# GpSimd's element operations written per block of 256 columns, in a decoder block whose recurrence runs on GpSimd

## The chip, the cores and the metric

One NeuronCore of a Trainium2 chip runs the whole kernel in one launch. The metric is the device time of one execution in microseconds (us). The engines are named as in the profile: PE is TensorE (PEld its weight load), DVE is VectorE, ACT is ScalarE, POOL is GpSimd, SP is SyncE, which here issues most DMAs. Each engine takes its own instructions in program order and waits on semaphores for the others.

## The reference, cut to what matters

```
x: 32 sequence steps x 256 tokens x 256 channels;  ctx: the same shape
# 1. attention stand-in: a complex recurrence along the 32 steps, per channel
c = exp(-exp(lmlg)) * exp(1j * theta)
state_n = c * state_(n-1) + x_n          # real part used
x = layernorm(x + Re(state) * x)
# 2. cross attention, 16 heads of 16 channels, over 256 context tokens
q = relu(x Wq + bq); k = relu(ctx Wk + bk); v = relu(ctx Wv + bv)
o = softmax(q k^T / 4) v + q
x = layernorm(x + ln_g * normalised(o) + ln_b)
# 3. eight experts; each token goes to the nearest of eight centroids
xn = rmsnorm(x) * scale; id = argmin |xn - centroid|^2
y = (a * silu(g)) down_w[id],  [a, g] = xn up_w[id]
out = layernorm(y + 2x)                  # skip inside the block and around it
```

## The kernel before, in words

A step handles one of the 32 sequence positions as an item of 256 tokens by 256 channels, held as [128 partitions, 2 token halves, 256 channels]; so most element operations have 512 columns. A first phase (recurrence, cross attention, routing) runs 37 software-pipelined steps, t = -2 to 34. In step t, GpSimd computes the recurrence for item t+3, PE and DVE do the scores and row maxima of item t, ACT the exponentials of item t-1, DVE the attention's division and norms of item t-2, and DVE, GpSimd and PE route item t-3 to its expert, with a scatter of its rows into buckets in DRAM. A second phase (`experts`, whose first tile DVE starts on at 868.0 us) loops over the buckets; the change doesn't touch it.

The order of the work is written out by hand: each engine has a `step(t)` that calls its pieces in a fixed order, DVE and PE and ACT along the heads h = 0 to 15. GpSimd's `step` is the list below line 772. In steady state, it runs:

1. the double product of the recurrence, `by_re` (L694): state times the pair of decays, 1024 columns;
2. `xw` (L752), the weighted row of item t-3, which ACT squares and sums into `nx`; then `x` plus the bias (L782);
3. `q_lo` (L770): q minus its rounded part `q_hi`, for the next item;
4. `dist<-cent_norm,nx` (L761, `offset`, 16 columns). DVE's `dist` (L1388, `pick` stage 0), the first step of the choice of an expert, waits for it;
5. the real part of the state (L702), two small norm instructions (L727, L729), the state's product (L710), `k_lo` (L770), the state's sum (L713), two more small ones;
6. the scatter's two indirect DMAs (L802), which wait for DVE's `slot` (L1425), the last step of the choice;
7. the state plus the new x (L720), then L727 and L729, for which DVE's `row` (L1258) waits, and four small ones (`rms`).

Two things hang on this list. DVE's `u` (L1266), `oq` (L1370) and `onehot_bf` (L1405) read two tiles of SBUF each and run while GpSimd works through points 1 to 5. And `k_lo` goes out to DRAM and comes back as `k_st` (SP, L585 and L586), which PE's first scores of the next item (L1004) wait for.

The GpSimd functions that the change touches, with line numbers as in the profile:

Of the kernel before, what the change touches and what calls it, by code (L numbers as in the profile page):

```python
# [5 lines left out]
F32 = mybir.dt.float32  # L6
# [4 lines left out]
ALU = mybir.AluOpType  # L11
# [3 lines left out]
P = 128  # L15
SEQ, TOK, C = 32, 256, 256
NCH = C // P
NTC = TOK // P
# [63 lines left out]
def build(nc, x, ctx_in, lmlg, theta, last_conv, Wq, bq, Wk, bk, Wv, bv, ln_g, ln_b, ffn_scale, centroids, up_w, down_w, out):  # L82
    stack = ExitStack()
    with stack:
        def sb(name, shape, dt=F32):
            return stack.enter_context(nc.sbuf_tensor(name, shape, dt))
# [4 lines left out]
        def sem(name):  # L91
            return stack.enter_context(nc.semaphore(name))
# [13 lines left out]
        scale_bc = sb("scale_bc", [P, C])  # L106
# [14 lines left out]
        def sb1(name, shape, dt=F32):  # L121
            return phase1.enter_context(nc.sbuf_tensor(name, shape, dt))

        state = sb1("state", [P, 2, NTC, C])
        by_re = sb1("by_re", [P, 2, NTC, C])
        xt = sb1("xt", [P, 2, NTC, C])
# [22 lines left out]
        x1 = sb1("x1", [P, 4, NTC, C])  # L149
# [6 lines left out]
        xw = sb1("xw", [P, NTC, C])  # L156
# [6 lines left out]
        b_bc = sb1("b_bc", [P, C])  # L163
        decay = sb1("decay", [P, 2, C])
        decay_im2, decay_re = decay[:, 0], decay[:, 1]
# [26 lines left out]
        row = sb1("row", [P, 2, NTC, ROWW])  # L192
# [33 lines left out]
        s = {n: sem(n) for n in names.split()}  # L226
# [36 lines left out]
        def active(item):  # L263
            return item.within(0, SEQ)
# [271 lines left out]
        with nc.Block() as block:  # L536
# [114 lines left out]
            def _(pool):  # L651
                g = nc.gpsimd
# [27 lines left out]
                pool.wait_ge(s["params"], PARAMS * 16)  # L680
                pool.wait_ge(s["setup_dve"], 11)

                both = [P, 2, NTC, C]
                re_b = decay_re.unsqueeze(1).to_broadcast([P, NTC, C])
                pair_b = decay[:, :, :].unsqueeze(2).to_broadcast(both)

                def conv_products(item):

                    if not active(item):
                        return  # L690
                    wait(pool, "conv", item - 1, 5)
                    if item.k == 1:
                        wait(pool, "x1_ok", item - 1, 2)
                    g.tensor_tensor(by_re[:, :, :, :], state[:, 0].unsqueeze(1).to_broadcast(both), pair_b, ALU.mult).then_inc(s["conv"], 1)  # L694

                def conv_real(item):

                    if not active(item):
                        return
                    wait(pool, "conv", item, 5, 1)  # L700
                    wait(pool, "u_ok", item - 1)
                    g.tensor_tensor(state[:, 0], by_re[:, 1], state[:, 1], ALU.subtract).then_inc(s["conv"], 1)  # L702

                def conv_imag(item, j):

                    if not active(item):
                        return
                    if j == 0:
                        wait(pool, "conv", item, 5, 2)
                        g.tensor_tensor(state[:, 1], state[:, 1], re_b, ALU.mult).then_inc(s["conv"], 1)  # L710
                    else:
                        wait(pool, "conv", item, 5, 3)
                        g.tensor_tensor(state[:, 1], state[:, 1], by_re[:, 0], ALU.add).then_inc(s["conv"], 1)  # L713

                def conv_input(item):
                    if not active(item):
                        return
                    wait_ring(pool, x_in[item.mod(2)], item, 2, 16)
                    wait(pool, "conv", item, 5, 4)
                    g.tensor_tensor(state[:, 0], state[:, 0], xt[:, item.mod(2)], ALU.add).then_inc(s["conv"], 1)  # L720

                def rstd(item, ready, per, mv, rs, done):

# [22 lines left out]
                def weigh(item):  # L746

                    if not active(item):
                        return
                    wait(pool, "x2_ok", item, 2)  # L750
                    wait(pool, "nx_ok", item - 1, 2)
                    g.tensor_tensor(xw[:, :, :], row[:, item.mod(2), :, 0:C], scale_bc[:, :].unsqueeze(1).to_broadcast([P, NTC, C]),  # L752
                                    ALU.mult).then_inc(s["xw_ok"], 1)

                def offset(item):

# [7 lines left out]
                def cut(item, src, hi, lo, ready, done, out):  # L764

                    if not active(item):
                        return
                    wait(pool, ready, item, 4)
                    wait_ring(pool, out[(item - 1).mod(2)], item - 1, 2, 32)
                    g.tensor_tensor(lo[:, :, :], src, hi[:, :, :].bitcast(F32), ALU.subtract).then_inc(s[done], 1)  # L770

                def step(t):
                    n, a, b = t + 1, t - 2, t - 3
                    first = t.k < 0
                    if first:
                        rstd(t + 2, "ln1", 4, mv1, rs1, "rstd1")
                    conv_products(t + 3)
                    weigh(b)
                    if active(a):
                        wait(pool, "x1_ok", a, 2)  # L780
                        wait(pool, "x1T_pe", a)
                        g.tensor_tensor(x1[:, a.mod(4)], x1[:, a.mod(4)], b_bc[:, :].unsqueeze(1).to_broadcast([P, NTC, C]),  # L782
                                        ALU.add).then_inc(s["x1b_ok"], 1)
                    if n.k > 0:
                        cut(n, q32[:, :, :], q_hi, q_lo, "q_ok", "q_cut", q_out)
                    offset(b)
                    conv_real(t + 3)
                    if not first:
                        rstd(t + 2, "ln1", 4, mv1, rs1, "rstd1")
                    conv_imag(t + 3, 0)  # L790
                    if n.k > 0:
                        cut(n, k32[:, :, :], k_hi, k_lo, "k_ok", "k_cut", k_out)
                    conv_imag(t + 3, 1)
                    rstd(a, "lnx", 4, mvx, rsx, "rstdx")
                    if active(b):

                        p = b.mod(2)
                        wait(pool, "slot_ok", b, SLOT)
                        wait(pool, "id_ok", b)
                        wait(pool, "rms", b, 4)  # L800
                        for c in range(NTC):
                            g.indirect_dma_start(out=buckets[:, :], out_offset=bass.IndirectOffsetOnAxis(ap=slot[:, p, c:c + 1], axis=0),  # L802
                                                 in_=row[:, p, c, :], in_offset=None, bounds_check=PAD - 1,
                                                 oob_is_err=False).then_inc(scat[p], 16)
                    conv_input(t + 3)
                    rstd(a, "ln2", 4, mv2, rs2, "rstd2")
                    rms(a)

                steps(pool, step)
                gpsimd2(pool)  # L810

# [648 lines left out]
```

## Time and profile before

| | |
|---|---|
| median of 3 runs | 1257.54 us (1252.96 to 1257.8) |
| the profiled execution's own time | 1257.0 us |
| its span, first to last instruction | 1255.2 us |
| PE busy | 1119.9 us (89%) |
| DVE busy | 942.7 us (75%) |
| POOL busy | 783.9 us (62%), 932 instructions |
| ACT busy | 669.9 us (53%) |

The span is what the profile's rows are measured in; 1.8 us lie around it. Shares are means over both phases: POOL is busy eight to nine tenths of the time through most of the first phase and three tenths in the second. A busy time of two neighbours on one engine can overlap by some hundredths of a microsecond, since an instruction's span begins when it is handed over; the distance from start to start is what one costs in a row of several.

### The profile page before, as it was taken

The numbers are of one execution on the slowest core, as the hardware profiler recorded it, in microseconds if no ns is written. First come the engines' busy times: TensorE is split into PE (matmuls) and PEld (weight loads), VectorE is DVE, ScalarE is ACT, GpSimd is POOL, SyncE is SP. The second block draws the span as 40 slices with busy tenths as digits, with TensorE's granted clock in tenths as the row PEclk, the third lists the DMA queues.
The fourth block names the chain that finished last, engine by engine and source line by source line (L and its number), as shares of the span: only waits on it lengthen the run. The fifth ranks groups of instructions, "written<-read, shape, count | busy, mean of one in ns | idle before, by whom it ended". The sixth has DMA issues, their size and how long they took to land.

```text
span 1255.2 us, 27516 instructions
## 1 busy us (share of the span) xinstructions
PE 1119.9 (89%) x8060; PEld 820.0 (65%) x8061; DVE 942.7 (75%) x2416; ACT 669.9 (53%) x1416; POOL 783.9 (62%) x932
## 2 busy tenths in 40 slices
PE   3799989999999998989999999752999999999996
PEld 2466666666666666656666666431888888888885
DVE  7558998988988998999898898763555555555553
ACT  4166776766667776767676777641222222222221
POOL 4637888888878988879888865561233333333333
PEclk9689999999989999999999999555999999999998
DMA  4676676665555565556556555042111111111110
GB/s 131 146 179 194 174 207 183 182 156 139 141 140 146 149 158 137 147 139 161 136 146 156 136 134 126 11 151 59 44 51 47 43 50 50 49 47 48 50 51 22
DMA packets 90826, 144.91 MB, mean 115 GB/s; under 512 B 12663, under 2 KB 78336, under 8 KB 84513
## 3 DMA queue, kind: packets, MB, share of 16 engines
q1 hardware_dynamic: 83616, 126.09, 38.6%
q0 software_dynamic: 6528, 16.99, 4.6%
q8 instruction: 55, 0.90, 0.3%
q10 hardware_dynamic: 576, 0.53, 0.2%
q14 instruction: 51, 0.41, 0.1%
HBM read 91.44 MB, written 53.03 MB: 115 GB/s over the span
## 4 chain that ended last, share of the span: by engine, by line
PE 45%; DVE 19%; POOL 15%; issue 10%; DMA 8%; SPq 2%; ACT 1%; POOLq 0%; DVEq 0%; ACTq 0%
PE Y L454 10%; PE G L422 8%; PE A L422 8%; DVE neg_max_sb L1243 7%; PE S L1004 3%; PE M L988 3%; DMA k_st<-k_pieces 3%; DMA k_pieces<-k_lo 3%; DVE oq L1370 3%; POOL buckets L802 2%; PE GT L432 2%; PE O L980 2%; POOL rs L729 2%; POOL by_re L694 2%; PE M L960 2%
## 5 line engine op out<-in xcount | busy, mean ns | idle before, releaser
L1243 DVE TENSOR_REDUCE neg_max_sb<-S 128x2 f32<-128x512 f32 x512 | 328.3, 682 | 71.0 <-PE S L1004 69.2
L864 ACT ACTIVATE probs<-T 128x512 f32<-128x512 f32 x512 | 277.9, 595 | 148.1 <-PE T L1017 136.8
L1004 PE MATMUL S<-k_st,q_st 48*128 48x256 f32 x1024 | 215.3, 321 | 46.3 <-DMA k_st<-k_pieces 27.8
L1004 PEld LDWEIGHTS S<-k_st,q_st 48*128 48x128 f32 x1024 | 147.3, 194 | 123.7 <-issue 53.5
L1017 PE MATMUL T<-q_st,k_st 49*128 49x256 f32 x1024 | 211.9, 321 | 9.8 <-ACT probs L864 8.1
L1017 PEld LDWEIGHTS T<-q_st,k_st 49*128 49x128 f32 x1024 | 148.0, 195 | 28.3 <-ACT probs L864 17.0
L399 ACT ACTIVATE gT<-GT 128x512 f32<-128x512 f32 x71 | 42.5, 599 | 209.4 <-PE GT L432 209.4
L980 PE MATMUL O<-probs,v_aug 128*32 128x256 f32 x2048 | 151.0, 416 | 0.7 <-ACT probs L864 0.7
L378 POOL DMA_INDIRECT out<-res,token x71 | 76.4, 1077 | 103.3 <-DVE res L499 98.8
L454 PE MATMUL Y<-dn_sb,gT 128*128 x568 | 134.2, 379 | 0.8 <-ACT gT L399 0.8
L802 POOL DMA_INDIRECT buckets<-row,slot x64 | 69.7, 1089 | 85.0 <-DVE slot L1425 74.8
L454 PEld LDWEIGHTS Y<-dn_sb,gT 128*128 128x128 f32 x568 | 107.5, 189 | 18.3 <-issue 1.0
L422 PE MATMUL G<-up_hi,xsT 128*128 x284 | 107.7, 420 | 1.2 <-DVE xsT L504 1.0
L422 PE MATMUL A<-up_hi,xsT 128*128 x284 | 107.1, 418 | 0.0
L383 POOL TENSOR_SCALAR rs<-mv 128x1 f32<-128x1 f32 x71 | 16.0, 226 | 142.4 <-DVE mv L528 142.2
L499 DVE TENSOR_SCALAR res<-y,mv,rs 128x256 f32<-128x256 f32 x71 | 29.4, 414 | 86.1 <-POOL rs L385 86.1
L980 PEld LDWEIGHTS O<-probs,v_aug 128*32 128x32 f32 x2048 | 56.5, 115 | 56.2 <-ACT probs L864 16.0
L694 POOL TENSOR_TENSOR by_re<-state,decay 128x1024 f32<-128x1024 f32 x31 | 73.4, 2366 | 1.2 <-DVE x L1330 0.9
L403 ACT ACTIVATE gate<-G 128x512 f32<-128x512 f32 x71 | 42.4, 597 | 58.7 <-PE G L422 58.7
L988 PE MATMUL M<-ctT,wk_sb 128*128 128x256 f32 x256 | 67.0, 407 | 6.1 <-issue 6.0
L1116 PE MATMUL M<-wv_sb,ctT 128*128 128x256 f32 x256 | 70.5, 399 | 0.0
L988 PE MATMUL M<-x1T,wq_sb 128*128 128x256 f32 x256 | 68.2, 411 | 0.8 <-ACT x1T L877 0.8
(184 smaller groups left out, 2541.1 us busy)
## 6 DMA issues: line engine op xcount, KB each, us to landing
q_st<-q_pieces SPq DMA_DIRECT2D x64, 256.0 KB
k_st<-k_pieces SPq DMA_DIRECT2D x64, 256.0 KB
xr<-buckets SPq DMA_DIRECT2D x71, 129.0 KB, 2.1
xt<-in_x SPq DMA_DIRECT2D x32, 256.0 KB, 6.3
ct<-in_ctx SPq DMA_DIRECT2D x32, 256.0 KB, 6.8
q_pieces<-q_hi SPq DMA_DIRECT2D x32, 256.0 KB, 2.1
q_pieces<-q_lo SPq DMA_DIRECT2D x32, 256.0 KB, 2.2
q_st<-q_pieces SPq DMA_DIRECT2D x64, 128.0 KB
```

The source lines that it names most:

```text
L378: g.indirect_dma_start(out=out_rows, out_offset=bass.IndirectOffsetOnAxis(ap=token[:, f.mod(2):f.mod(2) + 1], axis=0), in_=res[:, f.mod(2) ...
L422: last = t_.matmul(ps[:, :], xT[:, w, c * P:(c + 1) * P], src[:, bass.ds(off + c * 2 * HID, HID)], start=(k == 0), stop=(k == len(terms) - 1))
L454: last = t_.matmul(Y_ps[:, 0:C], gT[:, m.mod(2), c * P:(c + 1) * P], dn_sb[:, bass.ds(off + c * C, C)], start=(c == 0), stop=(c == HCH - 1))
L694: g.tensor_tensor(by_re[:, :, :, :], state[:, 0].unsqueeze(1).to_broadcast(both), pair_b, ALU.mult).then_inc(s["conv"], 1)
L802: g.indirect_dma_start(out=buckets[:, :], out_offset=bass.IndirectOffsetOnAxis(ap=slot[:, p, c:c + 1], axis=0), in_=row[:, p, c, :], in_of ...
L864: a_.activation(probs[:, h % 8].rearrange("p k t -> p (k t)"), T_ps[h % 2][:, :], ACT.Exp, scale=DH ** -0.5).then_inc(s["exp_ok"], 1)
L980: last = t_.matmul(O_ps[32 * j:32 * j + 32, (grp % 2) * TOK:(grp % 2 + 1) * TOK], v_aug[:, item.mod(4), kc, h * VW:h * VW + 32], probs[:, ...
L988: last = t_.matmul(dst[:, oc * TOK:(oc + 1) * TOK], w[:, ic, oc * P:(oc + 1) * P], xT[:, ic, :], start=(ic == 0), stop=(ic == NCH - 1))
L1004: last = t_.matmul(S_ps[h % 2][:, c * TOK:(c + 1) * TOK], q_st[base:base + STACK, h, c * P:(c + 1) * P], k_st[base:base + STACK, h, :], st ...
L1017: last = t_.matmul(T_ps[h % 2][:, c * TOK:(c + 1) * TOK], k_st[base:base + AUG, h, c * P:(c + 1) * P], q_st[base:base + AUG, h, :], start= ...
L1116: last = t_.matmul(M_ps[1][:, c * C:(c + 1) * C], ctT[:, ic, c * P:(c + 1) * P], wv_sb[:, ic, :], start=False, stop=(c == NTC - 1 and ic = ...
L1243: v.tensor_reduce(neg_max[:, cur.mod(2), :, h], S_ps[h % 2][:, :].rearrange("p (c t) -> p c t", c=NTC), AX.X, ALU.max, negate=True).then_i ...
```

## The change

Nine GpSimd operations of the first phase are each written as several instructions over 256 columns. The double product becomes four (two decays times two token halves), the other eight become two each. The semaphore is counted up by the last part alone, so who waits for whom stays. Operations, operands, their order and the other engines' programs stay. The small operations of 2 or 16 columns stay whole, and so do DVE's own copies of the recurrence for the first item.

```diff
-                both = [P, 2, NTC, C]
-                re_b = decay_re.unsqueeze(1).to_broadcast([P, NTC, C])
-                pair_b = decay[:, :, :].unsqueeze(2).to_broadcast(both)
...
-                    g.tensor_tensor(by_re[:, :, :, :], state[:, 0].unsqueeze(1).to_broadcast(both), pair_b, ALU.mult).then_inc(s["conv"], 1)
+                    for w in range(2):
+                        for c in range(NTC):
+                            last = g.tensor_tensor(by_re[:, w, c], state[:, 0, c], decay[:, w], ALU.mult)
+                    last.then_inc(s["conv"], 1)
...
-                    g.tensor_tensor(state[:, 0], by_re[:, 1], state[:, 1], ALU.subtract).then_inc(s["conv"], 1)
+                    for c in range(NTC):
+                        last = g.tensor_tensor(state[:, 0, c], by_re[:, 1, c], state[:, 1, c], ALU.subtract)
+                    last.then_inc(s["conv"], 1)
...
-                        g.tensor_tensor(state[:, 1], state[:, 1], re_b, ALU.mult).then_inc(s["conv"], 1)
+                        for c in range(NTC):
+                            last = g.tensor_tensor(state[:, 1, c], state[:, 1, c], decay_re, ALU.mult)
+                        last.then_inc(s["conv"], 1)
...
-                    g.tensor_tensor(lo[:, :, :], src, hi[:, :, :].bitcast(F32), ALU.subtract).then_inc(s[done], 1)
+                    for c in range(NCH):
+                        last = g.tensor_tensor(lo[:, c], src[:, c], hi[:, c].bitcast(F32), ALU.subtract)
+                    last.then_inc(s[done], 1)
...
```

The state's sum with `by_re` (L713), its sum with x (L720), `xw` (L752) and the bias (L782) are cut in the same way, by token half.

The order on GpSimd before, from the double product to the state's real part (points 1 to 5 of the list); the names in brackets are the semaphores that an instruction waits for:

```order
L694 TENSOR_TENSOR by_re<-state,decay 128x1024 [waits conv]
L752 TENSOR_TENSOR xw<-row,scale_bc 128x512 [waits nx_ok,x2_ok]
L782 TENSOR_TENSOR x<-x,b_bc 128x512 [waits x1T_pe,x1_ok]
L770 TENSOR_TENSOR q_lo<-q,q_hi 128x512 [waits q_out1,q_ok]
L761 TENSOR_TENSOR dist<-cent_norm,nx 128x16 [waits pick,nx_ok]
L702 TENSOR_TENSOR state<-by_re,state 128x512 [waits u_ok,conv]
```

The same place in the changed kernel (its line numbers run a little higher):

```order
L692 TENSOR_TENSOR by_re<-state,decay 128x256 [waits conv]
L692 TENSOR_TENSOR by_re<-state,decay 128x256 x3
L760 TENSOR_TENSOR xw<-row,scale_bc 128x256 [waits nx_ok,x2_ok]
L760 TENSOR_TENSOR xw<-row,scale_bc 128x256
L793 TENSOR_TENSOR x<-x,b_bc 128x256 [waits x1T_pe,x1_ok]
L793 TENSOR_TENSOR x<-x,b_bc 128x256
L779 TENSOR_TENSOR q_lo<-q,q_hi 128x256 [waits q_out1,q_ok]
L779 TENSOR_TENSOR q_lo<-q,q_hi 128x256
L769 TENSOR_TENSOR dist<-cent_norm,nx 128x16 [waits pick,nx_ok]
L702 TENSOR_TENSOR state<-by_re,state 128x256 [waits u_ok,conv]
L702 TENSOR_TENSOR state<-by_re,state 128x256
```

Four instructions in front of `dist` have become ten; the waits stand on the first part of each.

The order on GpSimd before, further on in the step, around `k_lo`:

```order
L710 TENSOR_TENSOR state<-state,decay 128x512 [waits conv]
L770 TENSOR_TENSOR k_lo<-k,k_hi 128x512 [waits k_out1,k_ok]
L713 TENSOR_TENSOR state<-state,by_re 128x512 [waits conv]
L727 TENSOR_SCALAR rsx<-mvx 128x2 [waits lnx]
L729 TENSOR_TENSOR rsx<-rsx,neg_half 128x2 [waits rstdx]
```

And after:

```order
L712 TENSOR_TENSOR state<-state,decay 128x256 [waits conv]
L712 TENSOR_TENSOR state<-state,decay 128x256
L779 TENSOR_TENSOR k_lo<-k,k_hi 128x256 [waits k_out1,k_ok]
L779 TENSOR_TENSOR k_lo<-k,k_hi 128x256
L717 TENSOR_TENSOR state<-state,by_re 128x256 [waits conv]
L717 TENSOR_TENSOR state<-state,by_re 128x256
L734 TENSOR_SCALAR rsx<-mvx 128x2 [waits lnx]
L736 TENSOR_TENSOR rsx<-rsx,neg_half 128x2 [waits rstdx]
```

Three instructions have become six. DVE's, PE's, ACT's and SP's orders are those of before.

## Rows read from the trace of the kernel before

**Rows 1.** Busy time of each engine in a stretch: us, PE, PEld, DVE, ACT, POOL, clock, DMA.

```profile
500.00:600.00 100.00, 92.67 (x828) 64.45 (x827) 95.10 (x242) 72.52 (x162) 84.90 (x94) 1.00 0.57 144
```

**Rows 2.** Timeline of POOL: start us, duration us; state plus x, two of 25.

```profile
158.18 1.30 POOL L720 TENSOR_TENSOR state<-state,xt 128x512 f32<-128x512 f32 x1
...
731.39 1.28 POOL L720 TENSOR_TENSOR state<-state,xt 128x512 f32<-128x512 f32 x1
```

**Rows 3.** Chain of waits, one step: start us, us, engine, what.

```profile
541.36 1.30 POOL state L720
...
543.69 0.74 DVE row L1258 x2
...
563.06 0.34 POOL buckets L802
...
565.45 1.29 POOL state L720
```

**Rows 4.** Timeline of POOL in that step.

```profile
545.29 2.37 POOL L694 TENSOR_TENSOR by_re<-state,decay 128x1024 f32<-128x1024 f32 x1
547.62 1.64 POOL L752 TENSOR_TENSOR xw<-row,scale_bc 128x512 f32<-128x512 f32 x1
...
550.45 1.28 POOL L770 TENSOR_TENSOR q_lo<-q,q_hi 128x512 fp32r<-128x512 f32 x1
551.68 0.22 POOL L761 TENSOR_TENSOR dist<-cent_norm,nx 128x16 f32<-128x16 f32 x1
551.85 1.28 POOL L702 TENSOR_TENSOR state<-by_re,state 128x512 f32<-128x512 f32 x1
...
554.67 1.29 POOL L710 TENSOR_TENSOR state<-state,decay 128x512 f32<-128x512 f32 x1
555.90 1.70 POOL L770 TENSOR_TENSOR k_lo<-k,k_hi 128x512 fp32r<-128x512 f32 x1
```

**Rows 5.** Timeline of DVE in that step.

```profile
545.68 2.53 DVE L1266 SCALAR_TENSOR_TENSOR u<-state,xt 128x512 f32<-128x512 f32 x1
...
552.04 0.36 DVE L1388 SCALAR_TENSOR_TENSOR dist<-M,row,dist 128x8 f32<-128x8 f32 x2
...
555.02 1.42 DVE L1370 TENSOR_TENSOR oq<-o,qn 128x256 f32<-128x256 f32 x1
556.38 1.25 DVE L1405 TENSOR_TENSOR onehot_bf<-expert_no,choice 128x16 bf16<-128x16 f32 x1
```

**Rows 6.** Two DVE lines over the run: ns min/median/max, first and last start.

```profile
L1266 DVE SCALAR_TENSOR_TENSOR u<-state,xt x32: 681/1705/2571, 14.0 to 736.1; 128x512 f32<-128x512 f32 x32
L1405 DVE TENSOR_TENSOR onehot_bf<-expert_no,choice x32: 155/176/1276, 126.4 to 853.3; 128x16 bf16<-128x16 f32 x32
```

**Rows 7.** The next step, which begins at 565.45: timelines of POOL and DVE.

```profile
575.78 0.21 POOL L761 TENSOR_TENSOR dist<-cent_norm,nx 128x16 f32<-128x16 f32 x1
580.21 0.20 DVE L1405 TENSOR_TENSOR onehot_bf<-expert_no,choice 128x16 bf16<-128x16 f32 x1
588.25 1.29 POOL L720 TENSOR_TENSOR state<-state,xt 128x512 f32<-128x512 f32 x1
```

**Rows 8.** A third kind of step (chain, PE, POOL), then who waited for whom.

```profile
483.00 1.66 POOL k_lo L770
493.35 0.50 PE S L1004 x2
504.74 0.22 POOL L761 TENSOR_TENSOR dist<-cent_norm,nx 128x16 f32<-128x16 f32 x1 [1.31 <-ACT junk L927]
PE S L1004 <- DMA k_st<-k_pieces: 19.7, 14, 2.1
POOL q_lo L770 <- ACT q L900: 31.7, 11, 11.8
```

**Rows 9.** Timeline of POOL at the start: two neighbours of one column.

```profile
0.34 0.09 POOL L1446 MEMSET const-float32-1.0<- 128x1 f32 x1
0.37 0.10 POOL L1446 MEMSET const-bfloat16-1.0<- 128x1 bf16 x1
```

More of the change, by code:

```diff
@@ L709, in conv_imag @@
                         wait(pool, "conv", item, 5, 2)
-                        g.tensor_tensor(state[:, 1], state[:, 1], re_b, ALU.mult).then_inc(s["conv"], 1)
+                        for c in range(NTC):
+                            last = g.tensor_tensor(state[:, 1, c], state[:, 1, c], decay_re, ALU.mult)
+                        last.then_inc(s["conv"], 1)
                     else:
                         wait(pool, "conv", item, 5, 3)
-                        g.tensor_tensor(state[:, 1], state[:, 1], by_re[:, 0], ALU.add).then_inc(s["conv"], 1)
+                        for c in range(NTC):
+                            last = g.tensor_tensor(state[:, 1, c], state[:, 1, c], by_re[:, 0, c], ALU.add)
+                        last.then_inc(s["conv"], 1)
                 def conv_input(item):
@@ L719, in conv_input @@
                     wait(pool, "conv", item, 5, 4)
-                    g.tensor_tensor(state[:, 0], state[:, 0], xt[:, item.mod(2)], ALU.add).then_inc(s["conv"], 1)
+                    for c in range(NTC):
+                        last = g.tensor_tensor(state[:, 0, c], state[:, 0, c], xt[:, item.mod(2), c], ALU.add)
+                    last.then_inc(s["conv"], 1)
                 def rstd(item, ready, per, mv, rs, done):
@@ L751, in weigh @@
                     wait(pool, "nx_ok", item - 1, 2)
-                    g.tensor_tensor(xw[:, :, :], row[:, item.mod(2), :, 0:C], scale_bc[:, :].unsqueeze(1).to_broadcast([P, NTC, C]),
-                                    ALU.mult).then_inc(s["xw_ok"], 1)
+                    for c in range(NTC):
+                        last = g.tensor_tensor(xw[:, c], row[:, item.mod(2), c, 0:C], scale_bc[:, :], ALU.mult)
+                    last.then_inc(s["xw_ok"], 1)
                 def offset(item):
@@ L781, in step @@
                         wait(pool, "x1T_pe", a)
-                        g.tensor_tensor(x1[:, a.mod(4)], x1[:, a.mod(4)], b_bc[:, :].unsqueeze(1).to_broadcast([P, NTC, C]),
-                                        ALU.add).then_inc(s["x1b_ok"], 1)
+                        for c in range(NTC):
+                            last = g.tensor_tensor(x1[:, a.mod(4), c], x1[:, a.mod(4), c], b_bc[:, :], ALU.add)
+                        last.then_inc(s["x1b_ok"], 1)
                     if n.k > 0:
```

## The prediction

> **What bounds the kernel now.** I read the busy times by stretch first, then the chain of waits, then one step on POOL and DVE instruction by instruction, and last the list of waits.
>
> In 100 us of the first phase PE is busy for 92.67, DVE for 95.10 and POOL for 84.90 at a granted clock of 1.00 [rows 1]: nobody is far from full, and only the chain can say who sets the pace. From 158.18 to 731.39 us there are 25 starts of the state plus x (L720), so 24 steps of 23.88 us on average [rows 2]. The chain in the step from 541.36 to 565.45 (24.09 us) runs from POOL's L720 over the two norm instructions to DVE's `row` (543.69), along DVE to the slot, then to POOL's scatter (563.06) and back to L720 [rows 3]. On the chain POOL counts only at the end, but its own rows show it tied with DVE: from L720 it works without a gap until `dist` ends at 551.90, 10.54 us after L720 [rows 4], and DVE's `dist`, which waits for it, starts at 552.04 [rows 5], no later than DVE's own work lets it. DVE is late there because `u` took 2.53 us for what takes 0.68 at best [rows 5, 6]: it started 0.4 us after `by_re` and ended (548.21) half a microsecond after `by_re` did (547.66) [rows 4, 5]. So a two-input DVE instruction doesn't run beside POOL's; it gets in at the boundary between two of them. Later `onehot_bf`, 0.155 us at best, took 1.25 in this step, ending at 557.63 with `k_lo` at 557.60.
>
> The Trainium skill has this as a rule (SBUF — State Buffer, "SBUF: two separate sides"): the port pair that the two share is locked for a whole instruction, and the loser blocks. The rows above agree, at 2.53 us against 0.68.
>
> Of the 24 steps, six look like this (mean 24.03). In nine `onehot_bf` wins the race against `k_lo` (0.20 us in the step from 565.45, ending 4.42 us after POOL's `dist` [rows 7]; in the first kind it is 5.73 [rows 4, 5]); they take 22.90 on average. From its end to the next L720 both kinds need the same: 7.84 and 7.82 us [rows 3, 5, 7]. The other nine (mean 24.78) begin with PE waiting for `k_st`, which is `k_lo` sent out and fetched back: `k_lo` ended at 484.66, the first scores came at 493.35, 8.7 us later [rows 8]. Fourteen such waits sum to 19.7 us [rows 8]. In this third kind POOL idles 1.31 us in front of its `dist` for ACT [rows 8].
>
> **The change, part by part.** Price of one more instruction: from start to start, `by_re` takes 2.33 us for 1024 columns, `q_lo` 1.23 for 512, `dist` 0.17 for 16 [rows 4]. So 512 columns more cost 1.10 (2.15 ns each), and what doesn't go with the columns is 1.23 - 512 x 0.00215 = 0.13 to 0.14; 0.17 - 16 x 0.00215 gives 0.14 too. `by_re` is a broadcast over three free dimensions, and its rate is that of the plain ones, so simpler operands should win nothing. I take 0.14 us. Below it stand the one-column memsets at a distance of 0.03 [rows 9], which read nothing; above, the 0.22 that a whole `dist` lasts [rows 4]. The chain adds 11 instructions a step (3 + 8 x 1), 1.5 us of POOL.
>
> The Trainium skill speaks against the change here (GPSIMD Engine Reference, § 7 "Performance pitfalls for Q7 kernels"): small read commands cost some 102 cycles each that don't pipeline. Two inputs at the 1.2 GHz that the page gives would make that an estimate of 0.17 us per part; no row separates a read command, and the sum by it would stand some 2 to 4 us higher.
>
> Where the parts lie: seven of the 11 (L720, three of `by_re`, `xw`, `x`, `q_lo`) stand between L720 and POOL's `dist`, where POOL has no gap: 7 x 0.14 = 0.98, so `dist` ends 11.52 us after L720 instead of 10.54. Bounds: 7 x 0.03 = 0.21 and 7 x 0.22 = 1.54.
>
> What DVE wins at `u`: it gets in after the first quarter of `by_re` instead of the fourth, some 1.5 us earlier. That is lost again 3 us on, since DVE's `dist` now waits for POOL's; and the time that `u` holds POOL up (`xw` 1.64 instead of 1.28 [rows 4]) only moves into `by_re`. I count it as nothing. Queued behind that wait on DVE are the division, `oq` and the next maxima, and behind those PE's scores.
>
> What DVE wins behind `dist`, counted from POOL's `dist`: before, L710 runs from 2.77 to 4.06, the second `oq` wants in at about 3.2, waits for that end and takes 0.5, and `onehot_bf` ends at 4.42 or 5.73 [rows 4, 5, 7]. After, the first half of L710 ends at about 3.6, `oq` at 4.1, and `onehot_bf` at 4.25 if it wins the race, or at 4.80 behind the second half of L710 (0.6). The middle is 4.5. The slot and the scatter follow 7.83 us later, as now. So a step that isn't held up by `k_st` takes 11.52 + 4.5 + 7.83 = 23.85 us (23.6 to 24.15): 0.2 less than the first kind, 0.95 more than the second.
>
> In the third kind the seven parts fit into POOL's 1.31 us of idling, DVE's work behind `dist` is taken as it was, and 24.78 becomes about 24.9 with what is left of L702, L710 and `k_lo` in front of the next scores. But there will be more of that kind. `k_lo` ends 16.2 us after L720 now (557.60 [rows 3, 4]); then at 11.52 + 6.05 = 17.6, which is 1.3 later, while the steps of the first two kinds grow by 0.5 on average. So `k_st` comes 0.8 us later against the scores. I take 13 steps of 24 for 9; the ends are 9 and all 24.
>
> Sum: 11 x 23.85 + 13 x 24.9 = 586.1 us against 573.2, or +13. With 9 late steps it is 581.9 (+9), with 24 it is 597.6 (+24). The steps before 158 us have POOL waiting for ACT's q, 31.7 us in eleven waits [rows 8], which swallows 1.5 us a step; the last steps wait for the slot, and the second phase has none of these instructions. I count nothing there. The profiled execution's own time is 1257.0 us, half a microsecond under the median of the runs (1257.54). Forecast: 1257 + 13 = 1270 us.
>
> **The rivals.**
> - *The extra instructions are nearly free.* Within a group no part waits for anything, and GpSimd may take the next as it takes memsets, at 0.03. Then steps of the first two kinds take 10.54 + 0.21 + 4.4 + 7.83 = 22.98, and the sum is 15 x 22.98 + 9 x 24.78 = 567.7, or -5.5; at no cost at all it is 15 x 22.77 + 223.0 = 564.6, or -8.6. That is 1248 to 1252; I name 1249, faster than before. It decides from where seven parts cost less than the onehot relief (6 steps x 1.2 and 9 x 0, 0.5 a step), which is 0.07 each. For it: the parts' missing waits. Against: `dist` and `xw` are handed over while their neighbour still runs, and still cost 0.14 beside their columns.
> - *The port stays with POOL through a group.* If DVE gets in only where a group ends, `u` waits for all of `by_re`, now 0.42 longer, and the race for `onehot_bf` is as before with groups 0.14 longer: 9 x 24.05 + 6 x 25.5 + 9 x 25.1 = 595.4, or +22; 1279 us, and up to 1285 with more late steps. Against it: between `by_re` and `xw`, which had nothing to wait for, `u` did get in [rows 4, 5].
> - *Nothing measurable.* The fetch of `k_st` has room for a `k_lo` that is later (only 14 waits, none over 2.1 us [rows 8]), no step turns into the third kind, and `onehot_bf` always wins its race: 15 x 23.6 + 223.0 = 577.0, or +4; 1261 us. Against it: 8.7 us of fetching is all that a step had left in the row shown.
>
> **How the numbers follow.** Chances: the forecast 0.5, the free parts 0.18, the kept port 0.12, nothing measurable 0.2. The forecast's own range is 1264 to 1282. Over all the cases 1250 to 1286 should hold the time 8 times in 10: it takes in most of the first rival and the kept port. About 0.5%, or 6.3 us, is what a measurement can tell from no change. Slower by more than that: the forecast and the kept port, 0.61; within it 0.21; faster 0.18.
>
> **What would show it.** Right: on POOL, start to start of 256-column parts of one group at 0.69 us (0.58 is the first rival); `u` at about 1 us where it was 2.5 (still 2.5 or more is the second); POOL's `dist` ending 11.5 us after L720, and DVE idling more than 1 us for it, where it idles for nothing now; no `onehot_bf` over 0.7 us; L720 to L720 at 23.85 where PE doesn't wait for `k_st`, and more than the 19.7 us of such waits in all. Wrong: L720 to L720 under 23.6 in most steps, or DVE not waiting for POOL's `dist`; then my reading of POOL as tied with DVE fell.

## The result and the profile after

| | before | after |
|---|---|---|
| median of 4 runs each, side by side | 1256.23 us | 1272.22 us (1264.78 to 1275.13) |
| ratio, 95% interval | | 1.0152 [1.0109, 1.0196] |
| the profiled execution | 1257.0 us | 1270.77 us |

The change makes the kernel 1.5% slower: +16 us by the medians, +13.8 us between the two profiled executions, where +13 was forecast. The profile's own head says that POOL's instructions grew from 932 to 1275, its busy time by 43.7 us, and that DVE's fell by 30:

```profile
span 1269.0 us, 27828 instructions
PE 1116.1 (88%) x8029; PEld 818.9 (65%) x8061; DVE 912.7 (72%) x2416; ACT 674.8 (53%) x1416; POOL 827.6 (65%) x1275
```

A DVE that is busy for less time is no gain here. One step on POOL in the kernel after (start us, us; in brackets the idle time ahead and who ended it) answers to [rows 4]; L726 is the old L720, L692 the double product, L712 and L717 the old L710 and L713:

```profile
601.14 1.43 POOL L726 TENSOR_TENSOR state<-state,xt 128x256 f32<-128x256 f32 x2
...
605.20 3.24 POOL L692 TENSOR_TENSOR by_re<-state,decay 128x256 f32<-128x256 f32 x4
608.41 1.32 POOL L760 TENSOR_TENSOR xw<-row,scale_bc 128x256 f32<-128x256 f32 x2
609.70 1.41 POOL L793 TENSOR_TENSOR x<-x,b_bc 128x256 f32<-128x256 f32 x2
611.07 1.41 POOL L779 TENSOR_TENSOR q_lo<-q,q_hi 128x256 fp32r<-128x256 f32 x2
612.45 0.21 POOL L769 TENSOR_TENSOR dist<-cent_norm,nx 128x16 f32<-128x16 f32 x1
612.62 1.41 POOL L702 TENSOR_TENSOR state<-by_re,state 128x256 f32<-128x256 f32 x2
614.01 0.21 POOL L734 TENSOR_SCALAR rs<-mv 128x2 f32<-128x2 f32 x1
614.30 0.94 POOL L736 TENSOR_TENSOR rs<-rs,neg_half 128x2 f32<-128x2 f32 x1
615.21 1.41 POOL L712 TENSOR_TENSOR state<-state,decay 128x256 f32<-128x256 f32 x2
616.59 1.83 POOL L779 TENSOR_TENSOR k_lo<-k,k_hi 128x256 fp32r<-128x256 f32 x2
...
625.57 1.42 POOL L726 TENSOR_TENSOR state<-state,xt 128x256 f32<-128x256 f32 x2
```

From start to start, `q_lo` costs 1.38 us where it cost 1.23: one part more, 0.15. `dist` ends at 612.66, 11.52 us after the step's start at 601.14, and no row up to it shows a wait. The same step on DVE, which answers to [rows 5]:

```profile
605.51 0.97 DVE L1277 SCALAR_TENSOR_TENSOR u<-state,xt 128x512 f32<-128x512 f32 x1
...
612.79 0.36 DVE L1399 SCALAR_TENSOR_TENSOR dist<-M,row,dist 128x8 f32<-128x8 f32 x2 [1.46 <-POOL dist L769]
...
615.95 1.17 DVE L1381 TENSOR_TENSOR oq<-o,qn 128x256 f32<-128x256 f32 x1
617.05 0.70 DVE L1416 TENSOR_TENSOR onehot_bf<-expert_no,choice 128x16 bf16<-128x16 f32 x1
```

`u` fell from 2.53 to 0.97 us, and DVE idles for 1.46 us in front of its `dist`, waiting for POOL's. The chain of waits of the kernel after (start us, us, what) says the same: from the step's start to `dist` it is now POOL's own row of instructions, where before it left POOL for DVE's `row` after 2.3 us [rows 3].

```profile
601.14 1.43 POOL state L726 x2
...
605.20 2.84 POOL by_re L692 x4
...
611.07 1.41 POOL q_lo L779 x2
612.48 0.18 POOL dist L769
...
612.79 0.36 DVE dist L1399 x2
...
617.12 0.63 DVE onehot_bf L1416
...
625.57 0.74 POOL state L726
```

Of the whole chain POOL has 23% where it had 15%, PE 41% where it had 45%. Who waited for whom, in the kernel after (us in total, times, longest; the first over the whole run, the second from 60 to 900 us):

```profile
DVE dist L1399 <- POOL dist L769: 29.5, 21, 3.5
PE S L1015 <- DMA k_st<-k_pieces: 26.6, 17, 3.6
```

In the kernel before the first of the two was this, of which nothing lay in the 24 steps:

```profile
DVE dist L1388 <- POOL dist L761: 6.9, 3, 3.4
```

The table below is worked out from the timelines of POOL and DVE, one profile of each kernel, over the 24 steps that the prediction counts. A step is cut in three, at the end of POOL's `dist` and at the end of `onehot_bf`. "Late" are steps in which POOL waits for ACT in front of its `dist` (the third kind); "lost" those in which `onehot_bf` took over 0.4 us, so that POOL got in ahead of it. The experiments stand beside the two kernels, for the sections below. The last column alone is counted from 60 to 900 us. The 23 runs of the kernel before that stand beside the last experiments spread over 19 us (1248.4 to 1267.1). If that lies in these steps, single profiles of one kernel can differ by some tenths of a microsecond a step, so a small difference between two rows says little.

| kernel | step, us | to `dist` | to `onehot_bf` | rest | late | lost | waits for `k_st`, us |
|---|---|---|---|---|---|---|---|
| before | 23.88 | 11.20 | 4.83 | 7.85 | 9 | 7 | 19.7 |
| after | 24.53 | 11.74 | 4.68 | 8.11 | 3 | 16 | 26.6 |
| product alone in four | 24.42 | 11.38 | 5.21 | 7.83 | 5 | 17 | 17.8 |
| product in two | 24.12 | 10.98 | 5.31 | 7.82 | 3 | 19 | 11.4 |
| only ahead of `dist` | 24.84 | 11.68 | 5.33 | 7.82 | 4 | 20 | 13.2 |
| only behind `dist` | 24.03 | 11.40 | 4.26 | 8.38 | 13 | 2 | 36.9 |
| delay alone | 24.71 | 11.40 | 5.48 | 7.82 | 4 | 21 | 17.4 |
| blocks of 128 | 26.38 | 13.45 | 4.59 | 8.34 | 5 | 12 | 62.9 |
| `k_lo` earlier | 23.81 | 10.99 | 4.96 | 7.86 | 6 | 7 | 15.5 |
| parts, `k_lo` earlier | 24.78 | 11.88 | 4.54 | 8.36 | 6 | 11 | 9.4 |

The 24 steps took 15.6 us longer (24 x 0.65): 13.0 of it up to `dist`, 6.2 in the rest, less 3.6 between. The run as a whole lost 13.8, so 2 us came back outside of them. Within the 24 steps PE's waits for `k_st` didn't grow: twelve of 18.2 us in all before, twelve of 17.8 after. The rise from 19.7 to 26.6 in the table lies outside of them.

### The profile page after: what moved, and what is told of

Read it like the earlier page. It is cut to its first block, busy times and chain, and to the rows that moved or that the text cites. A ratio compares the mean times of both kernels' runs of the same rounds, so it can differ in the third digit from the quotient of the medians.

```text
span 1269.0 us, 27828 instructions
## 1 busy us (share of the span) xinstructions
PE 1116.1 (88%) x8029; PEld 818.9 (65%) x8061; DVE 912.7 (72%) x2416; ACT 674.8 (53%) x1416; POOL 827.6 (65%) x1275
## 4 chain that ended last, share of the span: by engine, by line
PE 41%; POOL 23%; DVE 16%; issue 10%; DMA 6%; SPq 1%; ACT 1%; POOLq 0%; DVEq 0%; ACTq 0%
PE Y L454 10%; PE G L422 8%; PE A L422 8%; DVE neg_max_sb L1254 6%; POOL by_re L692 5%; PE M L999 3%; POOL buckets L813 3%; DMA k_st<-k_pieces 3%; DVE oq L1381 3%; PE GT L432 2%; PE S L1015 2%; POOL xw L760 2%; POOL state L726 2%; POOL q_lo L779 2%; POOL x L793 2%
## 5 line engine op out<-in xcount | busy, mean ns | idle before, releaser
L991 PE MATMUL O<-probs,v_aug 128*32 128x256 f32 x2048 | 153.7, 422 | 0.7 <-ACT probs L875 0.7
L692 POOL TENSOR_TENSOR by_re<-state,decay 128x256 f32<-128x256 f32 x124 | 97.4, 816 | 1.2 <-DVE x L1341 0.9
L991 PEld LDWEIGHTS O<-probs,v_aug 128*32 128x32 f32 x2048 | 57.0, 116 | 56.4 <-issue 15.6
```

The source lines that it names most:

```text
L692: last = g.tensor_tensor(by_re[:, w, c], state[:, 0, c], decay[:, w], ALU.mult)
L991: last = t_.matmul(O_ps[32 * j:32 * j + 32, (grp % 2) * TOK:(grp % 2 + 1) * TOK], v_aug[:, item.mod(4), kc, h * VW:h * VW + 32], probs[:, ...
```

## The experiments

The theory, from the prediction: POOL is tied with DVE, a part costs 0.14 us, and the parts ahead of `dist` set the loss. Rivals: that what DVE wins at `u` and `onehot_bf` outweighs it; that the later `k_lo`, through PE's waits for `k_st`, is what costs; that something in the split instructions themselves, their operands or the port, does. PE's clock is a fourth: over the 24 steps the granted clock was 0.97 before and 0.95 after. It was 0.98 in the experiment with the delay alone below, which lost three quarters as much, so a loss of that size needs no lower clock.

**The double product alone in four parts** (against the kernel before; the single instruction in its place goes):

```diff
+                    for w in range(2):
+                        for c in range(NTC):
+                            last = g.tensor_tensor(by_re[:, w, c], state[:, 0, c], decay[:, w], ALU.mult)
+                    last.then_inc(s["conv"], 1)
```

> The kernel before with the double product alone in four parts (three more instructions a step, the other operations whole). Theory (price of a part on POOL ahead of its `dist`): POOL's `dist` ends 10.54 + 3 x 0.14 = 10.96 us after the state plus x, DVE waits for it, `u` takes about 1 us, and 24 steps grow by 0.3 to 0.4 each: about 1264 us, ratio 1.006. Rival (DVE's gain at `u` is worth something by itself): 1250 us or less, ratio under 0.997, since this is the one part of the change that lets `u` in and it costs least. Second rival (only the fetch of `k_st` counts, by how late `k_lo` ends): a third of the whole change's loss, +5 us, with the steps that PE doesn't hold up unchanged at 22.9 and 24.0.

Measured: 1268.92 us, 1.0138 [1.0093, 1.0184]. Three parts of eleven make nearly the whole loss, more than twice what the theory had. `u` was relieved (0.90 us on average where it was 1.98), and the time rose all the same, so that gain won nothing that shows. Where POOL waits for nothing, `dist` ended 10.95 us into the step, 3 x 0.14 over 10.53. What the theory had not: `onehot_bf` lost its race against `k_lo` in 17 steps of 24, where it was 7.

**Only the operations behind `dist`**: the state's real part, product and sum and `k_lo` in halves, the rest as before.

```diff
-                    g.tensor_tensor(state[:, 0], by_re[:, 1], state[:, 1], ALU.subtract).then_inc(s["conv"], 1)
+                    for c in range(NTC):
+                        last = g.tensor_tensor(state[:, 0, c], by_re[:, 1, c], state[:, 1, c], ALU.subtract)
+                    last.then_inc(s["conv"], 1)
...
+                    if done == "k_cut":
+                        for c in range(NCH):
+                            last = g.tensor_tensor(lo[:, c], src[:, c], hi[:, c].bitcast(F32), ALU.subtract)
```

> The kernel before with only the operations behind POOL's `dist` in two parts (the state's real part, product and sum, and `k_lo`; four more instructions a step). Theory: `dist` still ends 10.54 us after the state plus x, so nothing is lost in front; `onehot_bf` ends 4.2 to 5.1 us after it in place of 4.4 or 5.7: between -8 and +2 us, ratio 0.994 to 1.002. Rival (the fetch of `k_st`): `k_lo` ends 0.4 us later, a third of the change's loss: +5 us, ratio 1.004, with more than 19.7 us of PE waits for `k_st`.

Measured: 1260.14 us, 1.0042 [1.0004, 1.0081]: over what the theory allowed, and at the rival's 1.004. Four parts behind `dist` cost little, and win nothing. `onehot_bf` ended 4.26 us after `dist` instead of 4.83 and lost only twice; the rest of the step took 8.38 instead of 7.85, and PE waited 36.9 us for `k_st` instead of 19.7. A step on DVE shows where the gain goes, in this experiment:

```profile
652.69 0.80 DVE L1381 TENSOR_TENSOR oq<-o,qn 128x256 f32<-128x256 f32 x1
653.42 0.16 DVE L1416 TENSOR_TENSOR onehot_bf<-expert_no,choice 128x16 bf16<-128x16 f32 x1
...
655.86 0.67 DVE L1388 SCALAR_TENSOR_TENSOR o<-oq,mvx,g_bc 128x256 f32<-128x256 f32 x1
...
656.53 0.63 DVE L1429 TENSOR_TENSOR place<-place,onehot_bf 128x16 f32<-128x16 f32 x1
```

and on POOL:

```profile
655.53 1.59 POOL L718 TENSOR_TENSOR state<-state,by_re 128x256 f32<-128x256 f32 x2
657.09 0.21 POOL L733 TENSOR_SCALAR rsx<-mvx 128x2 f32<-128x2 f32 x1
```

`onehot_bf` was through in 0.16 us, but an earlier DVE now meets the state's sum, which the parts ahead of it have pushed back. `o` waits for its first half, and `place`, 0.17 us at best, for its second (0.63, to 657.16). The slot follows `place`. What the kernel loses on top is the late steps, as the rival had it: 13 of 24.70 us where there were 9 of 24.78, beside 11 others of 23.25. With 9 late steps the 24 of this profile would have taken 571.1 us, 2 less than before.

**Only the operations ahead of `dist`** (against the kernel after; state's three operations and `k_lo` whole again):

```diff
+                    if done == "q_cut":
+                        for c in range(NCH):
+                            last = g.tensor_tensor(lo[:, c], src[:, c], hi[:, c].bitcast(F32), ALU.subtract)
+                    else:
+                        last = g.tensor_tensor(lo[:, :, :], src, hi[:, :, :].bitcast(F32), ALU.subtract)
```

> The changed kernel with the operations behind POOL's `dist` whole again (state's real part, product, sum, `k_lo`); the seven parts ahead of it stay. Theory: `dist` ends 11.5 us after the state plus x as in the changed kernel, and the whole loss stays: +13 to +18 us, ratio 1.010 to 1.014; if `onehot_bf` again takes 4.4 or 5.7 us after `dist`, a little over the changed kernel. Rival (the fetch of `k_st`): two thirds of the loss, +10 us. Rival (the parts behind `dist` cost the time, by what they do to the race for the port): no loss, ratio 1.00.

Measured: 1281.59 us, 1.0231 [1.0188, 1.0275]: more than expected, and slower than the whole change by its median, though the two intervals touch by 0.0008. The seven parts ahead of `dist` carry all of the loss; by the ratios the four behind it give about a third back. `dist` ended at 11.52 in steps where POOL waits for nothing, as in the kernel after, but `onehot_bf` lost in 20 steps, and a loss behind a whole `k_lo` costs 1.25 us:

```profile
618.02 1.35 DVE L1380 TENSOR_TENSOR oq<-o,qn 128x256 f32<-128x256 f32 x1
619.29 1.25 DVE L1415 TENSOR_TENSOR onehot_bf<-expert_no,choice 128x16 bf16<-128x16 f32 x1
```

In the kernel after it is 0.70 behind half of one. That is what the halves behind `dist` are good for.

**Blocks of 128 columns** (against the kernel after, every split operation once more in two):

```diff
-                            last = g.tensor_tensor(by_re[:, w, c], state[:, 0, c], decay[:, w], ALU.mult)
+                            for d in (0, P):
+                                last = g.tensor_tensor(by_re[:, w, c, d:d + P], state[:, 0, c, d:d + P], decay[:, w, d:d + P], ALU.mult)
```

> The changed kernel with every block of 256 columns cut into two of 128, so each suspected cost is doubled and more: 12 further instructions ahead of POOL's `dist`, 20 a step. Theory: `dist` ends at 11.5 + 12 x 0.14 = 13.2 us after the state plus x, steps take about 26.0 us, and the time is some 40 us over the changed kernel: about 1312 us, ratio to before 1.044. Rival (what counts is how long DVE is shut out): the blocks are half as long, so DVE gets in sooner and the time is no more than the changed kernel's, 1272 us or less.

Measured: 1326.73 us, 1.0601 [1.0552, 1.065]. 19 parts ahead of `dist` put its end at 13.26 us where POOL waits for nothing: (13.26 - 10.53) / 19 = 0.14, the same price as for 3 and 7. The loss is larger than the theory's: a step took 26.38 us where 26.0 was expected, which is 9 us in 24. The rest of the step, 8.34 us where the kernel before had 7.85, would be enough for that. PE's waits for `k_st` rise to 62.9 us as well, but only five steps are late; what they add isn't shown apart.

**The product in two**, one instruction per decay, so one part more ahead of `dist`:

```diff
+                    for w in range(2):
+                        last = g.tensor_tensor(by_re[:, w], state[:, 0], decay[:, w].unsqueeze(1).to_broadcast([P, NTC, C]), ALU.mult)
+                    last.then_inc(s["conv"], 1)
```

> The kernel before with the double product in two halves of 512 columns, one more instruction a step. Theory: `dist` ends at 10.54 + 0.14 = 10.68 us after the state plus x, `u` takes 1.2 to 1.9 us in place of 2.5, which helps nobody, and the time is 1 to 4 us over before, ratio 1.001 to 1.003 (up to 1.010 if the race for `onehot_bf` goes as in the first experiment). Rival (a quarter is too fine, but letting `u` in earlier is worth it): under 0.997.

Measured: 1262.73 us, 1.0033 [1.0, 1.0066]. One part is 0.15 us (`dist` at 10.68), and `onehot_bf` already loses in 19 steps; fewer late steps (3 for 9) pay for most of that.

**A delay with nothing split**: the kernel before, with three additions of 16 columns, into a tile that nobody reads, in front of `dist`.

```diff
+                    if active(b):
+                        for k in range(3):
+                            g.tensor_tensor(spare[:, k], expert_no[:, :, :], expert_no[:, :, :], ALU.add)
                     offset(b)
```

> The kernel before, every operation whole, with three small GpSimd instructions of 16 columns (a sum into a spare tile) put right in front of POOL's `dist`: 3 x 0.17 us there, and nothing else. Theory (later `dist` on POOL is what costs): `dist` ends at 11.05 us after the state plus x, DVE waits some 0.4 us for it in the steps that aren't late, and 24 steps grow by some 0.35 each: +8 us, ratio 1.005 to 1.008; if DVE starting right behind POOL also makes `onehot_bf` lose its race in nearly all of them, as in the first experiment, +13 to +17, ratio 1.010 to 1.014. Rival (DVE's own chain sets `dist`, and POOL's was only as late by chance): ratio 1.000 to 1.002, with no wait of DVE for POOL's `dist`.

Measured: 1273.41 us, 1.0111 [1.0071, 1.0152]. This tells delay from anything about the split itself: a delay alone is enough for a loss of this size, as the expectation had it for the case that the race is lost too. The three small instructions on POOL, and behind them DVE, in this experiment:

```profile
589.57 0.56 POOL L789 TENSOR_TENSOR spare<-expert_no 128x16 f32<-128x16 f32 x3
590.09 0.21 POOL L762 TENSOR_TENSOR dist<-cent_norm,nx 128x16 f32<-128x16 f32 x1
...
594.21 1.69 POOL L771 TENSOR_TENSOR k_lo<-k,k_hi 128x512 fp32r<-128x512 f32 x1
```

```profile
590.44 0.36 DVE L1392 SCALAR_TENSOR_TENSOR dist<-M,row,dist 128x8 f32<-128x8 f32 x2 [0.57 <-POOL dist L762]
...
594.68 1.25 DVE L1409 TENSOR_TENSOR onehot_bf<-expert_no,choice 128x16 bf16<-128x16 f32 x1
```

0.52 us more on POOL, and DVE waits for 0.57 us, with `u` not relieved (2.52 on average in steps that aren't late, 2.48 before). Nearly all steps that aren't late became alike: 24.49 us where they were 23.35, of which 0.52 is the delay and 0.65 the lost race. So half a microsecond on POOL costs 1.1 us in a step that isn't late, and 0.83 in the mean step, with no part of the recurrence split.

**`k_lo` one place earlier**, ahead of the state's product, in the kernel before and in the kernel after (the same edit):

```diff
-                    conv_imag(t + 3, 0)
                     if n.k > 0:
                         cut(n, k32[:, :, :], k_hi, k_lo, "k_ok", "k_cut", k_out)
+                    conv_imag(t + 3, 0)
```

> The kernel before with `k_lo` moved ahead of the state's product (L710), nothing cut. `k_lo` ends up to 1.28 us earlier unless it then waits for ACT's k. Theory of the fetch (late steps are those whose `k_st` comes late): the 19.7 us of waits for `k_st` shrink by half, five of the nine late steps become ordinary ones of 23.35: -7 us, ratio 0.992 to 0.998. Rival (late steps are only the other side of the short ones; POOL's stretch and DVE set the mean): ratio 0.998 to 1.004 though the waits shrink.

> The changed kernel with `k_lo` moved ahead of the state's product, all parts kept. Only 3 of 24 steps of the changed kernel are late by ACT, but it has 26.6 us of waits for `k_st`. Theory (the later `dist` and not `k_lo` makes the loss): 1266 to 1272 us, ratio 1.008 to 1.014, `dist` still ending at 11.5 us. Rival (the later `k_lo` makes it): the loss vanishes, 1255 to 1260 us.

Measured: before with the edit 1259.16 us, 1.0012 [0.9983, 1.0041]; after with it 1276.13, 1.0143 [1.0107, 1.0179]. The second is the one that tells: PE's waits for `k_st` went down to a third,

```profile
PE S L1015 <- DMA k_st<-k_pieces: 9.4, 7, 2.1
```

and the loss stayed. So the later `k_lo` is not what the change costs; the gain that the theory of the fetch expected in the kernel before didn't come, and its rival's range held (0.998 to 1.004). With only the parts behind `dist`, the late steps above say, the fetch does cost something.

**`onehot_bf` with one tile as input**: two instructions, one per token half, with the choice as a scalar column instead of a second tile, in the kernel before; and together with the double product in four.

```diff
-                        v.tensor_tensor(onehot_bf[:, :, :], expert_no[:, :, :], ch, ALU.is_equal).then_inc(s["pick"], 1)
+                        for c in range(NTC):
+                            last = v.tensor_scalar(onehot_bf[:, c], expert_no[:, c], choice[:, c:c + 1], None, ALU.is_equal)
+                        last.then_inc(s["pick"], 1)
```

> The kernel before with `onehot_bf` written as two DVE instructions that read one tile and a scalar column each, so that it reads only one tile of SBUF and needn't race GpSimd. Theory (the race costs 1.1 to 1.3 us in each step that `onehot_bf` loses): the seven long ones of 24 steps go, two short instructions of some 0.1 us come: 24 steps lose 5 to 8 us, ratio 0.993 to 0.997, unless more steps then wait for `k_st`. Rival (the race hides behind something else): ratio 1.000 and more, by the added instruction.

> The double product in four parts as in the first experiment, and `onehot_bf` with one tile input. The first experiment cost 13 to 17 us where 3 x 0.14 us in some 19 steps make 8; its trace has 17 of 24 steps with a long `onehot_bf` against 7 before. Theory (that lost race is the rest): the time falls to the time of before with `onehot_bf` of one input plus 8, about 1257 us, ratio 1.001, with POOL's `dist` still ending 10.96 us after the state plus x. Rival (the rest of the loss has another cause): 1265 us or more stays.

Measured: 1298.60 us, 1.0358 [1.0302, 1.0414]; with the product in four 1306.65, 1.0405 [1.035, 1.0459]. Both were meant to take the race away and did the opposite. DVE in the first of the two:

```profile
556.91 2.49 DVE L1406 TENSOR_SCALAR onehot_bf<-expert_no,choice 128x8 bf16<-128x8 f32 x2
```

and POOL:

```profile
556.46 1.69 POOL L770 TENSOR_TENSOR k_lo<-k,k_hi 128x512 fp32r<-128x512 f32 x1
558.12 1.26 POOL L713 TENSOR_TENSOR state<-state,by_re 128x512 f32<-128x512 f32 x1
```

Two instructions of eight columns ended at 559.40, each behind a whole one of POOL: `k_lo` (to 558.15) and the state's sum (to 559.38). They lost in every step, so the pair can't say what the product would cost with the race gone. That stays open.

**The double product moved behind `dist`**, whole in the kernel before and in four parts in the kernel after:

```diff
-                    conv_products(t + 3)
                     weigh(b)
...
                     offset(b)
+                    conv_products(t + 3)
                     conv_real(t + 3)
```

> The kernel before, all operations whole, with the double product moved behind POOL's `dist` (it is needed only by the state's real part, which follows). Theory (POOL's gapless stretch from the state plus x to `dist` and DVE's lock behind the double product set DVE's `dist`): `dist` ends some 8.2 us after the state plus x or as soon as ACT's `nx` is there, DVE reaches it at about 10, and steps not held up by `k_st` take 22.3 to 23.0 in place of 23.35; `k_lo` ends where it did, so more steps begin with PE waiting for `k_st`: 1243 to 1256 us, ratio 0.990 to 1.000. Rival (the fetch of `k_st` sets the mean step): ratio 1.000 or more and more than 19.7 us of waits for `k_st`.

> The changed kernel, all parts kept, with the double product moved behind POOL's `dist`. The parts and their price stay on POOL, 11 a step; only four parts of the seven stay ahead of `dist`, and 2.8 us of double product go. Theory (what costs is the parts' place ahead of `dist`): most of the loss vanishes, 1252 to 1262 us, ratio 0.997 to 1.005, with what is left in steps that wait for `k_st`, since `k_lo` still ends 17.3 us or more after the state plus x. Rival (what costs is POOL's total work, wherever it stands): 1270 us and more stays.

Measured: 1324.85 us, 1.0538 [1.0479, 1.0598], and 1365.85, 1.0889 [1.0833, 1.0946]. The first was expected faster than the kernel before, the second about as fast; they are my worst misses. POOL with the whole product:

```profile
548.20 0.21 POOL L761 TENSOR_TENSOR dist<-cent_norm,nx 128x16 f32<-128x16 f32 x1 [1.31 <-ACT junk L927]
548.37 2.40 POOL L694 TENSOR_TENSOR by_re<-state,decay 128x1024 f32<-128x1024 f32 x1
```

and DVE:

```profile
549.70 1.10 DVE L1395 TENSOR_TENSOR cand<-dist,least 128x16 f32<-128x16 f32 x1
550.72 0.63 DVE L1370 TENSOR_TENSOR oq<-o,qn 128x256 f32<-128x256 f32 x1
551.27 1.24 DVE L1399 SCALAR_TENSOR_TENSOR cand<-cand,expert_no 128x16 f32<-128x16 f32 x1
```

The 2.3 us that went from in front of `dist` had covered ACT's sums (`nx`), which come no earlier: POOL now waits 1.31 us for them in all 24 steps. And the product lies where DVE makes its choice: one `cand` of 16 columns waits for it, the next for the state's real part right behind it, and `onehot_bf` ends 7.91 us after `dist`. In four parts that becomes 5.27, the one place where the halving pays as meant (2.6 us), but the rest takes 9.50, since `place` and `o` now meet the halves of `k_lo` and of the state's sum, and PE waits 81.8 us for `k_st`.

No kernel tried was faster than the one before.

## Why the prediction was right, and where it was lucky

*A part costs 0.14 us, start to start.* Right. In steps where POOL waits for nothing, `dist` ends 10.53, 10.68, 10.95, 11.53 and 13.26 us into the step with 0, 1, 3, 7 and 19 parts: 0.14 to 0.15 each. The first rival (parts nearly free) fell with it. The three additions of 16 columns cost 0.17 each, or 0.14 without their columns (16 x 2.15 ns). By the Trainium skill (GPSIMD Engine Reference, § 7 "Performance pitfalls for Q7 kernels") the prediction had an estimate of 0.17 for a part; the rows put it at 0.14.

*`dist` 11.52 us after L720.* Right to 0.01. *`u` relieved, and worth nothing.* Right: 0.91 us on average where it was 1.98, and DVE then idled for 20.6 us in front of its `dist` in the 24 steps, where it idled for nothing. The second rival (the port kept through a group) needed `u` at 2.5 or more and fell too: DVE gets in between two parts.

*`onehot_bf` 4.5 us after `dist`, then 7.83.* The term that was mis-sized: 24.34 us for a step that isn't late, where 23.85 was forecast. In 11 of those 21 steps, of which the step from 601.14 is one, the second `oq` asks (there at 615.95) when the first half of L712 has just handed over to the second; I had that boundary at 3.6 us after `dist`, and it came at about 3.24 (615.21 + 1.38 / 2 - 612.66). So `oq` waits for the second half, `onehot_bf` then loses against the first half of `k_lo`, and ends at 5.10, outside of 4.25 to 4.80. These steps take 24.44. The boundary came early because the two small norm instructions ahead of L712 took 1.20 us there (614.01 to 615.21). In the step of the kernel before that I had worked from they took 1.58, up to L710 at 554.67:

```profile
553.09 0.82 POOL L727 TENSOR_SCALAR rs<-mv 128x2 f32<-128x2 f32 x1
553.99 0.71 POOL L729 TENSOR_TENSOR rs<-rs,neg_half 128x2 f32<-128x2 f32 x1
```

In the other ten `onehot_bf` ends at 4.35 on average, but then `o` and `place` meet the state's sum, as in the experiment with only the parts behind `dist`, and the rest is 8.35 on average instead of 7.83: 24.23 us. "The slot and the scatter follow 7.83 us later, as now" is the sentence that failed; I had counted the delay of what stands behind `dist` on POOL for `k_st` only, not for DVE's last stretch. That no `onehot_bf` is over 0.7 us held within hundredths (0.70 to 0.79 where it loses).

*13 late steps of 24.9.* Wrong, and this made up for the term above: 3 steps of 25.88. The 19.7 us of waits for `k_st` that I read were counted from 60 to 900 us, and they rose to 26.6 as said, but not in the steps that I had counted: there it was twelve waits before and after. And a late fetch makes a late step less often: before, nine of those twelve did, after, three. A step of the kernel after that isn't late, on PE, DVE and POOL:

```profile
379.91 0.50 PE L1015 MATMUL S<-k_st,q_st 48*128 48x256 f32 x2 [1.43 <-DMA k_st<-k_pieces]
```

```profile
384.62 0.98 DVE L1277 SCALAR_TENSOR_TENSOR u<-state,xt 128x512 f32<-128x512 f32 x1
...
391.22 0.36 DVE L1399 SCALAR_TENSOR_TENSOR dist<-M,row,dist 128x8 f32<-128x8 f32 x2 [0.71 <-POOL dist L769]
```

```profile
379.58 1.42 POOL L726 TENSOR_TENSOR state<-state,xt 128x256 f32<-128x256 f32 x2
...
390.88 0.20 POOL L769 TENSOR_TENSOR dist<-cent_norm,nx 128x16 f32<-128x16 f32 x1
```

PE stood 1.43 us for `k_st`, and `u` came 5.04 us after the step's start, 0.67 later than in the step from 601.14. Still POOL's `dist` was on time, and DVE idled 0.71 us for it instead of 1.46: its idle time took the wait in. I had moved the fetch against the scores, and not moved the point from which it counts. The sum, with counts and sizes as they came: 21 x 24.34 + 3 x 25.88 = 588.8 us against 573.2, and 586.1 forecast. With the right steps and my 13 late ones it would have been 591.4, with my steps and the right count 575.6. The delay on POOL was right in place and size. That the sum came within 3 us is luck: a step sized half a microsecond too short and a count of late steps that went the other way than forecast offset each other.

*What the prediction didn't have*: that a delay of POOL sends `onehot_bf` into losing. Before, it lost in 7 of 24 steps. In the five kernels in which DVE waits for POOL's `dist` in 16 to 21 of the steps it lost in 16 to 21, whatever made the delay; with blocks of 128, and with the parts and `k_lo` earlier, DVE waits in 13 and 9, and it lost in 12 and 11. DVE, released by POOL, then comes to the boundaries of L710 and `k_lo` in the same position each time. By the profiles this is why half a microsecond costs one in the experiment with the delay alone, where the two kinds of [rows 5, 7] became one. No experiment shows it by itself, for the pair that should have taken the race away made it worse. What decides the single race is open: in the kernel before, two steps with the same times up to `oq`, within 0.02 us, ended differently (from 277.54 and from 517.28 us).

The rival "nothing measurable" rested on room in the fetch of `k_st`. There was room, and the loss came all the same.

## What to carry to other kernels

Splitting one engine's instructions so that another gets at a shared port earlier can pay only where the engine that is split has time left. Here POOL had none up to its `dist`, 0.14 us a part went straight into the step, and what DVE won it spent waiting for POOL. Where two engines are tied, look at the handover that both reach together, and price a delay by a small dummy instruction in front of it before any rewriting: three additions of 16 columns made three quarters of the loss of the whole change (1.0111 of 1.0152). And when an operation is moved away from in front of a wait, ask first what it was covering.

## What the runs showed of the hardware

- An instruction of DVE with one tile and a scalar column (TENSOR_SCALAR, 128x8 f32 to bf16) is held up by POOL's as much as one with two tiles, in the kernel with `onehot_bf` in that form (ns min/median/max):

```profile
L1406 DVE TENSOR_SCALAR onehot_bf<-expert_no,choice x64: 219/1264/1320, 126.2 to 893.2; 128x8 bf16<-128x8 f32 x64
```

I had expected it to run beside POOL. The Trainium skill (SBUF — State Buffer, "Who interferes with whom") has a DVE instruction with at most one SBUF input outside the 2-port modes free of contention, and lets `tensor_scalar` enter such modes; the median of 1264 ns says only that this one contends, not by which way. In the 24 steps, 47 of the 48 ended within 0.04 us of the end of an instruction of POOL.
- The wait goes by POOL's instruction, not by DVE's: two-tile instructions of 16 columns took 1.25 us behind a whole `k_lo` and 0.70 behind half of one, and the one-tile ones of 8 columns took 1.26 in the median, behind whole ones.
- POOL lets DVE in between two of its instructions that have nothing to wait for: `u` took 0.90 us on average with the product alone in four parts, 1.98 with it whole.
